# A graph kernel's edge sort with two half-float values per edge in place of one packed whole number in fp32

## The chip, the cores and the metric

One core of one Trainium2 chip runs the kernel. The metric is the device time of one execution in microseconds (us). A timed measurement is the median of several runs. TensorE (PE in the rows; PEld is its weight loading), VectorE (DVE), ScalarE (ACT), GpSimd (POOL) and SyncE (SP, which only issues transfers here) run side by side and meet at semaphores.

## What is computed

Four graph layers over 625 nodes of 512 features and 10625 edges (source, destination, a type 0 or 1, 64 edge features), each behind a layer norm and a ReLU, each added to x. The change touches only how the edges are brought into order by destination for the first two layers:

```python
def rgcn_gate_layer(x, row, col, edge_type, basis, att, gate_w, root, bias):
    w = jnp.einsum('rb,bio->rio', att, basis)
    x_j = x[col]
    ...
    msg = jnp.where((edge_type == 0)[:, None], msgs[0], msgs[1])
    agg = jax.ops.segment_sum(msg, row, num_segments=x.shape[0])
    return agg + x @ root + bias
x = x + _L0_gnn_ref(h, edge_index, edge_type_2, ...)   # two such layers, 30 basis matrices each
x = x + _L1_gnn_ref(h, edge_index, ...)                # GCN
x = x + _L2_gnn_ref(h, edge_index, edge_attr_64, ...)  # MLP per edge
x = x + _L3_gnn_ref(h, edge_index_t, ...)              # MLP per edge, no edge features
```

## The kernel before

The first phase (to about 465 us of the trace) does the two gated layers and the GCN. The sums over edges become products with count matrices (how many edges of a type go from node m to node n), and these are built on the chip in two steps.

**The sort.** The edges lie in 84 tiles of 128. DVE finds for each edge its place among the edges ordered by chunk of 128 destinations: a tile (0 to 87) and a slot in it (0 to 127). Then 84 fp32 matmuls move one number per edge there: for edge tile e the stationary operand `place_hots[e % 24]` (128x128, GpSimd, L716) has a one at the edge's slot, the moving operand `value_hots[e % VALUE_RING]` (128x88, DVE, `move_hots`, L740) has the edge's number in the column of its tile. All 84 add up in one PSUM bank, `PS[:, MOVE_BANK, 0:88]` (`sort`, L350). The number packs all three values: (1024 * type + source) * 256 + destination in the chunk + 1 (`places`, L788 to L794). `read_moved` (L743 to L758) takes it apart with seven DVE operations. `VALUE_RING` is 21 slots, in the space of `is_src`.

**The counting.** For each of the 87 sorted tiles DVE writes `is_slot` (128x128, L764) and `is_src` (128x640, L766) in half-float, and PE multiplies them (L369, L371).

**The order around it** is written by hand, one program per engine:

- PE runs `sort(0)` to `sort(83)`. After e = 2, 6, ..., 78 comes a `mix` (L393): four 32-column fp32 matmuls that combine the 30 basis matrices of layer 1 by one of 56 pieces of 1 MB. After e = 45, 49, ..., 61 there are four transposes of a chunk of the normed input (L399); after e = 67 the gates, `gates` (L405, 20 matmuls with 2 columns); after e = 73 and e = 80 a product with `root` (`product`, L411). Then come `clear` (L364) and the counting.
- DVE runs `move_hots(0)` to `move_hots(83)`, with other work put in after fixed e: the norm's statistics after 28, the normed rows after 36, `slots(0)` after 46, `chunks(1)` after 56, `pack_chunks` after 60, `places_without_gaps` after 66, `pairs_of_chunks` after 72, `chunks(0)` after 76 (L1061 to L1079).
- GpSimd writes the 84 `place_hots` and waits only for a free one of 24.
- ACT copies the mixes out of PSUM (L1272). SP loads piece n when mix n - 4 has ended (`load`, L610).

Of the kernel before, what the change touches and what calls it, by code (L numbers as in the profile page):

```python
# [8 lines left out]
F32 = mybir.dt.float32  # L9
F32R = mybir.dt.float32r  # L10
BF16 = mybir.dt.bfloat16
FP16 = mybir.dt.float16
# [5 lines left out]
P = 128  # L18
# [24 lines left out]
KIND = 1024.0  # L43
SPOT = 256.0
LOW = 1
# [6 lines left out]
def gnn_stack(nc, a, out):  # L52
    ctx = ExitStack()
    with ctx:
# [129 lines left out]
        with early:  # L184
# [52 lines left out]
            group_id = part(10)  # L237
            values = part(11)[:, 0:ET]
            by_chunk = part(12).rearrange("p (j t) -> p j t", j=4)
# [52 lines left out]
            PLACE_RING = 24  # L292
            VALUE_RING = HOT * NP // 2 // SC
            place_hots = packed[:].rearrange("p c n -> p (c n)")[:, 0:PLACE_RING * P].rearrange("p (b n) -> p b n", n=P)
            value_hots = is_src[:].rearrange("p b n -> p (b n)").bitcast(F32)[:, 0:VALUE_RING * SC].rearrange("p (b n) -> p b n", n=SC)
            EARLY_BANKS = (7, 0, 1)
# [26 lines left out]
            def _(pe):  # L323
# [22 lines left out]
                def sort(e):  # L346

                    pe.wait_ge(sem("place_hots"), e + 1)
                    pe.wait_ge(sem("one_hot"), e + 1)
                    nc.tensor.matmul(PS[:, MOVE_BANK, 0:SC], place_hots[:, e % PLACE_RING, :], value_hots[:, e % VALUE_RING, :],  # L350
                                     start=(e == 0), stop=(e == ET - 1), skip_group_check=True).then_inc(sem("hot_used"), 1)

                def clear(g):

                    if g:
                        pe.wait_ge(sem("packing"), NT * g)
                        pe.wait_ge(sem("packed"), NT * g)
                    else:
                        pe.wait_ge(sem("zeros"), 1)
                        pe.wait_ge(sem("rank_read"), 2)  # L360
                        pe.wait_ge(sem("by_chunk"), 7)
                        pe.wait_ge(sem("side_ev"), EARLY_SIDES)
# [4 lines left out]
                def count(t, c):  # L367
                    pe.wait_ge(sem("one_hot"), ET + 2 * t + 2)
                    nc.tensor.matmul(PS[:, bass.ds(c, 1), :].rearrange("p c o -> p (c o)"), is_slot[:, t % HOT, :], is_src[:, t % HOT, 0:512],  # L369
# [365 lines left out]
            def _(dve):  # L735
                def move_hots(e):

                    if e >= VALUE_RING:
                        dve.wait_ge(sem("hot_used"), e - VALUE_RING + 1)
                    nc.vector.tensor_scalar(value_hots[:, e % VALUE_RING, :], node_of_col[:, 0:SC], slot_tile[:, 1, e:e + 1],  # L740
                                            values[:, e:e + 1], ALU.is_equal, ALU.mult).then_inc(sem("one_hot"), 1)

                def read_moved():  # L743

                    moved = PS[:, MOVE_BANK, 0:SC]
                    dst_s, kind_s, src_s, weight_s = (by_chunk[:, j, :] for j in range(4))
                    dve.wait_ge(sem("hot_used"), ET)
                    nc.vector.tensor_scalar(src_s, moved, 1.0 / SPOT, -0.25, ALU.mult, ALU.add).then_inc(sem("by_chunk"), 1)
                    dve.wait_ge(sem("by_chunk"), 1)
                    nc.vector.tensor_scalar(src_s, src_s, ROUND, -ROUND, ALU.add, ALU.add).then_inc(sem("by_chunk"), 1)  # L750
                    dve.wait_ge(sem("by_chunk"), 2)
                    nc.vector.scalar_tensor_tensor(dst_s, src_s, -SPOT, moved, ALU.mult, ALU.add).then_inc(sem("by_chunk"), 1)
                    nc.vector.tensor_scalar(kind_s, src_s, KIND, None, ALU.is_ge).then_inc(sem("by_chunk"), 1)
                    dve.wait_ge(sem("by_chunk"), 4)
                    nc.vector.tensor_scalar(dst_s, dst_s, -1.0, None, ALU.add).then_inc(sem("by_chunk"), 1)
                    nc.vector.scalar_tensor_tensor(src_s, kind_s, -KIND, src_s, ALU.mult, ALU.add).then_inc(sem("by_chunk"), 1)
                    nc.vector.tensor_scalar(weight_s, kind_s, PACK - 1.0, 1.0, ALU.mult, ALU.add).then_inc(sem("by_chunk"), 1)
                    dve.wait_ge(sem("by_chunk"), 7)  # L758

# [26 lines left out]
                def places():  # L786

                    nc.vector.scalar_tensor_tensor(place[:], group, -float(P), ends[:], ALU.mult, ALU.add).then_inc(sem("place"), 1)  # L788
                    nc.vector.scalar_tensor_tensor(values, kind[:], KIND, ends[:, 0, :], ALU.mult, ALU.add).then_inc(sem("place"), 1)
                    dve.wait_ge(sem("place"), 2)  # L790
                    nc.vector.scalar_tensor_tensor(values, values, SPOT, place[:, 1, :], ALU.mult, ALU.add).then_inc(sem("values"), 1)
                    dve.wait_ge(sem("values"), 1)
                    nc.vector.tensor_scalar(values, values, 1.0, None, ALU.add).then_inc(sem("values"), 1)
                    dve.wait_ge(sem("values"), 2)  # L794

# [1416 lines left out]
```

## Time and profile before

| | us |
|---|---|
| median of 3 runs (lowest to highest) | 1159.91 (1156.43 to 1161.3) |
| the profiled execution's own time | 1161.15 |
| its span in the trace | 1159.4 |
| PE busy in the span | 1086.1 (94%) |
| DVE busy | 835.8 (72%) |
| GpSimd busy | 559.3 (48%) |
| first sort matmul to the first operation of `read_moved` | 25.4 to 103.7 |

The page of the profile lists busy times over the span, a table of slices, and the costliest groups. A row of the timeline gives the start, the time until the last of the merged instructions ended, the engine, the line, out<-in with shapes, the count, and in brackets the idle time of the engine before it with what ended it. An fp32 matmul stands in the trace as two PE records and two PEld records, a half-float one as one of each, so `L350 ... x8` is four sorts.

### The profile page before, as it was taken

The page shows a single profiled execution, that of the slowest core. Times are in us where ns is not written, and L with a number is a line of the kernel's source. Part 1 is how long each engine was busy: PE and PEld are TensorE (multiplying, and loading weights), DVE is VectorE, ACT ScalarE, POOL GpSimd, SP SyncE. Part 2 cuts the span into 40 slices and gives each one's busy share as a digit, 9 for nine tenths or more (in the row PEclk, how much of TensorE's full clock was granted, in tenths as well). Part 3 has the DMA queues.
Part 4 walks back from the last instruction along what each step waited for, and adds up shares of the span by engine and source line. Part 5 has one row for each costly group of instructions (what it writes and reads, how often), then busy time and mean ns, then how long its engine had stood idle before and what let it go on. Part 6 is the DMA issues. An engine that isn't in the chain of part 4 may idle for free. (4 is left out here: it accounts for less than half of the span.)

```text
span 1159.4 us, 15448 instructions
## 1 busy us (share of the span) xinstructions
PE 1086.1 (94%) x4410; PEld 607.0 (52%) x4442; DVE 835.8 (72%) x1852; ACT 558.3 (48%) x978; POOL 559.3 (48%) x518
## 2 busy tenths in 40 slices
PE   3989888899999989899999999999999999999997
PEld 1564222344557453655565565555555557446664
DVE  5694677769755153688788788788888867849997
ACT  0221321310332221477777777777777744116663
POOL 1960112233433330667876666666666300027774
PEclk9988989999999999899999999999999999999999
DMA  7995997657211005595554454445454010026665
GB/s 283 341 404 212 360 400 264 231 184 233 84 48 46 13 14 194 132 259 111 114 110 92 101 98 95 100 95 97 98 98 88 1 55 23 9 93 197 203 206 173
DMA packets 60182, 172.66 MB, mean 149 GB/s; under 512 B 12645, under 2 KB 13189, under 8 KB 52552
## 3 DMA queue, kind: packets, MB, share of 16 engines
q0 software_dynamic: 31536, 72.01, 26.6%
q1 hardware_dynamic: 28568, 99.66, 23.4%
q8 instruction: 42, 0.69, 0.2%
q14 instruction: 36, 0.29, 0.1%
HBM read 159.65 MB, written 11.98 MB: 148 GB/s over the span
## 5 line engine op out<-in xcount | busy, mean ns | idle before, releaser
L1664 PE MATMUL PS<-wide,hidT 128*128 128x512 f32 x672 | 302.1, 592 | 2.2 <-DVE hidT L1540 0.4
L705 POOL DMA_INDIRECT rec_scratch<-rec_src,slot_row x84 | 102.5, 1220 | 252.8 <-DMA rec_scratch<-rec_src,slot_row 208.2
L1664 PEld LDWEIGHTS PS<-wide,hidT 128*128 128x128 f32 x672 | 128.6, 191 | 122.8 <-issue 120.5
L1482 POOL DMA_INDIRECT pair_sum<-table_j,counts_rec x84 | 136.7, 1627 | 27.3 <-issue 25.3
L1598 ACT ACTIVATE wide<-PS 128x512 f32<-128x512 f32 x168 | 100.5, 598 | 99.6 <-PE PS L1648 63.5
L1801 POOL DMA_INDIRECT u_space<-table_j,wide x87 | 86.1, 990 | 108.7 <-DMA table_j<-agg_space 81.8
L1474 POOL DMA_INDIRECT pair_sum<-table_i,counts_rec x84 | 89.5, 1066 | 98.9 <-PE PS L1648 59.5
L1603 ACT ACTIVATE wide<-wide,two 128x512 f32<-128x512 f32 x168 | 120.9, 720 | 6.2 <-DVE wide L1533 6.2
L1533 DVE SCALAR_TENSOR_TENSOR wide<-wide 128x512 f32<-128x512 f32 x168 | 116.4, 693 | 5.8
L1491 POOL DMA_INDIRECT rec_scratch<-rec_src,slot_row x84 | 89.5, 1066 | 40.9 <-issue 21.6
L1608 ACT ACTIVATE wide<-wide 128x512 f32<-128x512 f32 x168 | 105.8, 630 | 5.3
L1540 DVE SCALAR_TENSOR_TENSOR hidT<-wide,PS 128x512 f32<-128x512 f32 x84 | 57.8, 688 | 54.0 <-ACT wide L1608 54.0
L1272 ACT COPY pieces<-PS 128x512 f32<-128x512 f32 x56 | 32.8, 586 | 122.4 <-PE PS L393 122.4
L393 PE MATMUL PS<-pieces,mixer 128*32 128x512 f32 x448 | 67.8, 683 | 22.6 <-DVE mixer L1053 13.8
L1648 PE MATMUL PS<-attr,w_attr 128*128 128x128 f32 x672 | 88.7, 275 | 0.0
L1531 DVE TENSOR_SCALAR wide<-wide 128x512 f32<-128x512 f32 x168 | 72.2, 430 | 20.9 <-ACT wide L1598 20.9
L1648 PEld LDWEIGHTS PS<-attr,w_attr 128*128 128x128 f32 x672 | 81.6, 192 | 0.0
L411 PE MATMUL PS<-w_rel,hT 128*128 128x512 f32 x160 | 71.7, 598 | 1.8 <-ACT pieces L1272 1.8
L1885 DVE TENSOR_TENSOR wide<-PS,u_space 128x512 f32<-128x512 f32 x87 | 59.9, 689 | 10.1 <-issue 4.3
L1553 DVE SCALAR_TENSOR_TENSOR mes<-wide,PS 128x512 f32<-128x512 f32 x84 | 57.8, 688 | 12.2 <-ACT wide L1608 2.7
L1645 PEld LDWEIGHTS PS<-ident,pair_sum 128*128 128x128 f32 x336 | 41.7, 140 | 44.3 <-issue 44.3
L716 POOL TENSOR_SCALAR packed<-node_of_col,wide 128x128 f32<-128x128 f16 x84 | 51.0, 631 | 23.3 <-DVE wide L862 23.3
(325 smaller groups left out, 1884.9 us busy)
## 6 DMA issues: line engine op xcount, KB each, us to landing
pieces<-basis_rows SPq DMA_DIRECT2D x56, 1024.0 KB, 7.5
ring<-basis_low SPq DMA_DIRECT2D x30, 256.0 KB, 6.4
w_scratch<-pieces SPq DMA_DIRECT2D x112, 32.0 KB
counts_rec<-rec_scratch SPq DMA_DIRECT2D x1, 2856.0 KB, 9.8
rec_scratch<-rec_src,slot_row POOLq DMA_INDIRECT x168, 2.3
root<-L_gnn_root SPq DMA_DIRECT2D x2, 1024.0 KB, 8.0
rows_in<-in_rows_in SPq DMA_DIRECT2D x2, 1024.0 KB, 13.9
w_rel<-w_scratch SPq DMA_DIRECT2D x1, 2048.0 KB, 11.6
```

What stands on the lines that cost most here:

```text
L705: nc.gpsimd.indirect_dma_start(out=rec3_dram, out_offset=bass.IndirectOffsetOnAxis(ap=slot_row[:, 1, t:t + 1], axis=0), in_=rec, in_offset ...
L1474: nc.gpsimd.indirect_dma_start(out=pair_sum[:, t % GOT3, :], out_offset=None, in_=tables[0][0], in_offset=bass.IndirectOffsetOnAxis(ap=idx ...
L1482: nc.gpsimd.indirect_dma_start(out=pair_sum[:, t % GOT3, :], out_offset=None, in_=tables[0][1], in_offset=bass.IndirectOffsetOnAxis(ap=idx ...
L1491: nc.gpsimd.indirect_dma_start(out=rec5_dram, out_offset=bass.IndirectOffsetOnAxis(ap=slot_row[:, 0, t:t + 1], axis=0), in_=rec5_src[:, t, ...
L1531: nc.vector.tensor_scalar(u, u, CLAMP, None, ALU.min).then_inc(sem(f"clamp{l}"), 1)
L1533: nc.vector.scalar_tensor_tensor(u, u, 2.0, u, ALU.add, ALU.mult).then_inc(sem(f"top{l}"), 1)
L1598: nc.scalar.activation(grow[l][:, t % 2, :], PS[:, bank, :], ACT.Exp).then_inc(sem(f"exp{l}"), 1)
L1603: nc.scalar.activation(u, u, ACT.Ln, bias=two[:]).then_inc(sem(f"ln{l}"), 1)
L1608: nc.scalar.activation(u, u, ACT.Exp, scale=-1.0).then_inc(sem(f"inv{l}"), 1)
L1648: m = nc.tensor.matmul(PS[:, pre_bank(t), k * P:(k + 1) * P], w_attr[:, k * P:(k + 1) * P], attr[:, t * P:(t + 1) * P], start=False, stop= ...
L1664: m = nc.tensor.matmul(o, hidT[:, t % 2, k * P:(k + 1) * P], w2[:, k, :], start=False, stop=(k == KT - 1), skip_group_check=True)
L1801: nc.gpsimd.indirect_dma_start(out=got5[:, t % GOT5, :], out_offset=None, in_=tables[1][1], in_offset=bass.IndirectOffsetOnAxis(ap=rec5[:, ...
```

## The change

`values` holds two rows per edge: row 0 is destination in the chunk + 1, row 1 is 1024 * type + source. Both are whole numbers that a half-float holds exactly. `value_hots` becomes half-float with 2 x 88 columns per edge tile, and `move_hots` writes the two halves with two instructions (L740 each); `VALUE_RING` stays 21. `place_hots` becomes half-float in the same bytes' space, written by the same 84 GpSimd instructions. `sort` becomes one half-float matmul with 176 moving columns in place of an fp32 one with 88. `read_moved` goes from seven operations to four, `places` from four to three. The semaphore counts follow.

```diff
@@ -41,7 +41,6 @@
 KIND = 1024.0
-SPOT = 256.0
 LOW = 1
@@ -235,7 +234,7 @@
             group_id = part(10)
-            values = part(11)[:, 0:ET]
+            values = part(11).rearrange("p (j t) -> p j t", j=2)
             by_chunk = part(12).rearrange("p (j t) -> p j t", j=4)
@@ -290,9 +289,9 @@
             PLACE_RING = 24
-            VALUE_RING = HOT * NP // 2 // SC
-            place_hots = packed[:].rearrange("p c n -> p (c n)")[:, 0:PLACE_RING * P].rearrange("p (b n) -> p b n", n=P)
-            value_hots = is_src[:].rearrange("p b n -> p (b n)").bitcast(F32)[:, 0:VALUE_RING * SC].rearrange("p (b n) -> p b n", n=SC)
+            VALUE_RING = HOT * NP // (2 * SC)
+            place_hots = packed[:].rearrange("p c n -> p (c n)").bitcast(FP16)[:, 0:PLACE_RING * P].rearrange("p (b n) -> p b n", n=P)
+            value_hots = is_src[:].rearrange("p b n -> p (b n)")[:, 0:VALUE_RING * 2 * SC].rearrange("p (b n) -> p b n", n=2 * SC)
             EARLY_BANKS = (7, 0, 1)
@@ -346,8 +345,8 @@
                     pe.wait_ge(sem("place_hots"), e + 1)
-                    pe.wait_ge(sem("one_hot"), e + 1)
-                    nc.tensor.matmul(PS[:, MOVE_BANK, 0:SC], place_hots[:, e % PLACE_RING, :], value_hots[:, e % VALUE_RING, :],
+                    pe.wait_ge(sem("one_hot"), 2 * e + 2)
+                    nc.tensor.matmul(PS[:, MOVE_BANK, 0:2 * SC], place_hots[:, e % PLACE_RING, :], value_hots[:, e % VALUE_RING, :],
                                      start=(e == 0), stop=(e == ET - 1), skip_group_check=True).then_inc(sem("hot_used"), 1)
@@ -358,14 +357,14 @@
                         pe.wait_ge(sem("rank_read"), 2)
-                        pe.wait_ge(sem("by_chunk"), 7)
+                        pe.wait_ge(sem("by_chunk"), 4)
                         pe.wait_ge(sem("side_ev"), EARLY_SIDES)
...
                 def count(t, c):
-                    pe.wait_ge(sem("one_hot"), ET + 2 * t + 2)
+                    pe.wait_ge(sem("one_hot"), 2 * ET + 2 * t + 2)
                     nc.tensor.matmul(PS[:, bass.ds(c, 1), :].rearrange("p c o -> p (c o)"), is_slot[:, t % HOT, :], is_src[:, t % HOT, 0:512],
@@ -737,25 +736,21 @@
                         dve.wait_ge(sem("hot_used"), e - VALUE_RING + 1)
-                    nc.vector.tensor_scalar(value_hots[:, e % VALUE_RING, :], node_of_col[:, 0:SC], slot_tile[:, 1, e:e + 1],
-                                            values[:, e:e + 1], ALU.is_equal, ALU.mult).then_inc(sem("one_hot"), 1)
+                    for j in range(2):
+                        nc.vector.tensor_scalar(value_hots[:, e % VALUE_RING, SC * j:SC * (j + 1)], node_of_col[:, 0:SC], slot_tile[:, 1, e:e + 1],
+                                                values[:, j, e:e + 1], ALU.is_equal, ALU.mult).then_inc(sem("one_hot"), 1)
...
-                    moved = PS[:, MOVE_BANK, 0:SC]
+                    moved = PS[:, MOVE_BANK, 0:2 * SC].rearrange("p (j t) -> p j t", j=2)
                     dst_s, kind_s, src_s, weight_s = (by_chunk[:, j, :] for j in range(4))
                     dve.wait_ge(sem("hot_used"), ET)
-                    nc.vector.tensor_scalar(src_s, moved, 1.0 / SPOT, -0.25, ALU.mult, ALU.add).then_inc(sem("by_chunk"), 1)
-                    dve.wait_ge(sem("by_chunk"), 1)
-                    nc.vector.tensor_scalar(src_s, src_s, ROUND, -ROUND, ALU.add, ALU.add).then_inc(sem("by_chunk"), 1)
+                    nc.vector.tensor_scalar(kind_s, moved[:, 1, :], KIND, None, ALU.is_ge).then_inc(sem("by_chunk"), 1)
+                    nc.vector.tensor_scalar(dst_s, moved[:, 0, :], -1.0, None, ALU.add).then_inc(sem("by_chunk"), 1)
                     dve.wait_ge(sem("by_chunk"), 2)
-                    nc.vector.scalar_tensor_tensor(dst_s, src_s, -SPOT, moved, ALU.mult, ALU.add).then_inc(sem("by_chunk"), 1)
-                    nc.vector.tensor_scalar(kind_s, src_s, KIND, None, ALU.is_ge).then_inc(sem("by_chunk"), 1)
+                    nc.vector.scalar_tensor_tensor(src_s, kind_s, -KIND, moved[:, 1, :], ALU.mult, ALU.add).then_inc(sem("by_chunk"), 1)
+                    nc.vector.tensor_scalar(weight_s, kind_s, PACK - 1.0, 1.0, ALU.mult, ALU.add).then_inc(sem("by_chunk"), 1)
                     dve.wait_ge(sem("by_chunk"), 4)
-                    nc.vector.tensor_scalar(dst_s, dst_s, -1.0, None, ALU.add).then_inc(sem("by_chunk"), 1)
-                    nc.vector.scalar_tensor_tensor(src_s, kind_s, -KIND, src_s, ALU.mult, ALU.add).then_inc(sem("by_chunk"), 1)
-                    nc.vector.tensor_scalar(weight_s, kind_s, PACK - 1.0, 1.0, ALU.mult, ALU.add).then_inc(sem("by_chunk"), 1)
-                    dve.wait_ge(sem("by_chunk"), 7)
@@ -786,12 +781,10 @@
                     nc.vector.scalar_tensor_tensor(place[:], group, -float(P), ends[:], ALU.mult, ALU.add).then_inc(sem("place"), 1)
-                    nc.vector.scalar_tensor_tensor(values, kind[:], KIND, ends[:, 0, :], ALU.mult, ALU.add).then_inc(sem("place"), 1)
+                    nc.vector.scalar_tensor_tensor(values[:, 1, :], kind[:], KIND, ends[:, 0, :], ALU.mult, ALU.add).then_inc(sem("place"), 1)
                     dve.wait_ge(sem("place"), 2)
-                    nc.vector.scalar_tensor_tensor(values, values, SPOT, place[:, 1, :], ALU.mult, ALU.add).then_inc(sem("values"), 1)
+                    nc.vector.tensor_scalar(values[:, 0, :], place[:, 1, :], 1.0, None, ALU.add).then_inc(sem("values"), 1)
                     dve.wait_ge(sem("values"), 1)
-                    nc.vector.tensor_scalar(values, values, 1.0, None, ALU.add).then_inc(sem("values"), 1)
-                    dve.wait_ge(sem("values"), 2)
```

On DVE the order stays, with two instructions where one stood. The place is the stretch from the 57th edge tile to the 73rd, around the other work that the prediction speaks of; L740 is `move_hots`, L980/L973 is `chunks(1)`, L809/L802 is `pack_chunks`, L873 to L896 (now L866 to L889) is `places_without_gaps`. Before:

```order
58 L980 SCALAR_TENSOR_TENSOR wide<-slot_of_col,wide 128x88 x3
59 L740 TENSOR_SCALAR is_src<-node_of_col,wide 128x88 x4
60 L807 COPY wide<-wide 128x11
61 L809 SCALAR_TENSOR_TENSOR wide<-wide 128x11 x7
62 L811 CAST words<-wide 1x11
63 L740 TENSOR_SCALAR is_src<-node_of_col,wide 128x88 x6
64 L873 MEMSET wide 128x6
```

With the change:

```order
57 L973 SCALAR_TENSOR_TENSOR wide<-slot_of_col,wide 128x88 x3
58 L740 TENSOR_SCALAR is_src<-node_of_col,wide 128x88 x8
59 L800 COPY wide<-wide 128x11
60 L802 SCALAR_TENSOR_TENSOR wide<-wide 128x11 x7
61 L804 CAST words<-wide 1x11
62 L740 TENSOR_SCALAR is_src<-node_of_col,wide 128x88 x12
63 L866 MEMSET wide 128x6
```

Four and six instructions became eight and twelve; nothing else moved.

On PE the order stays too. The place is the end of the sort, from the sort of e = 67 over the gates to the last one (L350/L349 `sort`, L405/L404 `gates`, L393/L392 `mix`, L411/L410 the root product). Before:

```order
52 L350 MATMUL PS<-is_src,packed 128x88
53 L405 MATMUL PS<-gate_cols,hT 128x2 x20
54 L350 MATMUL PS<-is_src,packed 128x88 x3
55 L393 MATMUL PS<-pieces,mixer 32x512 x4
56 L350 MATMUL PS<-is_src,packed 128x88 x3
57 L411 MATMUL PS<-root,hT 128x512 x4
```

With the change:

```order
52 L349 MATMUL PS<-is_src,packed 128x176
53 L404 MATMUL PS<-gate_cols,hT 128x2 x20
54 L349 MATMUL PS<-is_src,packed 128x176 x3
55 L392 MATMUL PS<-pieces,mixer 32x512 x4
56 L349 MATMUL PS<-is_src,packed 128x176 x3
57 L410 MATMUL PS<-root,hT 128x512 x4
```

The sorts have twice the columns in the same places.

## Rows read from the trace of the kernel before

**Rows 1.** The page: busy time of each engine over the span.
```profile
PE 1086.1 (94%) x4410; PEld 607.0 (52%) x4442; DVE 835.8 (72%) x1852; ACT 558.3 (48%) x978; POOL 559.3 (48%) x518
```

**Rows 2.** Stages: stretch, us, busy PE PEld DVE ACT POOL (last rows PE), PEclk, DMA, GB/s.
```profile
24.60:78.60 54.00, 45.19 (x292) 25.75 (x293) 42.53 (x143) 12.77 (x24) 51.73 (x85) 0.97 0.91 356
...
86.40:93.00 6.60, 6.60 (x24) 0.50 0.55 185
93.00:103.70 10.70, 10.70 (x51) 1.00 0.67 247
```

**Rows 3.** Timeline, DVE and POOL: the value and place one-hots.
```profile
24.58 8.15 DVE L740 TENSOR_SCALAR is_src<-node_of_col,wide 128x88 f32<-128x88 f16 x28
26.55 6.94 POOL L716 TENSOR_SCALAR packed<-node_of_col,wide 128x128 f32<-128x128 f16 x12
...
59.97 15.77 POOL L716 TENSOR_SCALAR packed<-node_of_col,wide 128x128 f32<-128x128 f16 x26
...
84.79 1.72 DVE L740 TENSOR_SCALAR is_src<-node_of_col,wide 128x88 f32<-128x88 f16 x7
```

**Rows 4.** DVE's busy time in the stretches of other work between the one-hots.
```profile
33.96:37.48 3.52, 3.49 (x13) 1.00 0.86 283
48.88:52.86 3.98, 3.84 (x10) 1.00 1.01 418
55.73:61.50 5.77, 5.29 (x16) 1.00 1.04 418
64.40:65.83 1.43, 1.29 (x5) 0.54 1.04 433
67.05:69.33 2.28, 2.00 (x10) 1.00 1.01 419
71.05:76.52 5.47, 4.94 (x17) 1.00 1.02 419
```

**Rows 5.** Timeline, PE and DVE: the last sorts and what follows them.
```profile
48.88 0.17 DVE L105 TENSOR_TENSOR small<-small 128x5 f32<-128x5 f32 x1 [8.39 <-ACT small L135]
...
77.39 1.06 PE L393 MATMUL PS<-pieces,mixer 128*32 128x512 f32 x8 [2.79 <-DMA pieces<-basis_rows]
...
78.67 7.97 PE L405 MATMUL PS<-gate_cols,hT 128*128 128x2 f32 x40
...
86.51 1.56 PE L350 MATMUL PS<-is_src,packed 128*128 128x88 f32 x6
...
91.24 4.51 PE L411 MATMUL PS<-root,hT 128*128 128x512 f32 x8
...
96.87 1.12 PE L350 MATMUL PS<-is_src,packed 128*128 128x88 f32 x8
...
99.44 3.63 PE L411 MATMUL PS<-root,hT 128*128 128x512 f32 x8
...
103.74 0.25 DVE L748 TENSOR_SCALAR wide<-PS 128x88 f32<-128x88 f32 x1 [17.23 <-PE PS L350]
```

**Rows 6.** Timeline, DVE and PE: half-float one-hots, and half-float matmuls.
```profile
105.18 0.25 DVE L764 TENSOR_SCALAR is_slot<-node_of_col,wide 128x128 f16<-128x128 f16 x1
105.35 0.44 DVE L766 TENSOR_SCALAR is_src<-node_of_col,wide 128x640 f16<-128x640 f16 x1
...
105.70 0.25 DVE L764 TENSOR_SCALAR is_slot<-node_of_col,wide 128x128 f16<-128x128 f16 x1
...
137.05 0.38 PE L369 MATMUL PS<-is_src,is_slot 128*128 128x512 f16 x1
...
137.32 0.38 PE L369 MATMUL PS<-is_src,is_slot 128*128 128x512 f16 x1
```

**Rows 7.** Groups by line: GpSimd beside the normed rows (48 to 53 us), and its memsets.
```profile
L716 POOL TENSOR_SCALAR packed<-node_of_col,wide 128x128 f32<-128x128 f16 x7 | 5.2, 773 | 0.0
...
L1795 POOL MEMSET none<- 128x512 bf16 x1 | 0.5, 547 | 0.0
L709 POOL MEMSET x_rows<- 128x512 f32 x1 | 0.5, 525 | 0.3 <-POOLq L2204 0.3
```

## The prediction

> **What bounds the kernel now.** I read the busy times first [rows 1]: PE is busy 94% of the span, so time won or lost where PE stands or works in the early stages mostly arrives at the end. Then the stages [rows 2]: in the first 54 us of the sort PE is busy 45.2 us, DVE 42.5 and GpSimd 51.7, with the DMA engines at 0.91. No single engine is the bound there, so the order of the program decides. The timeline of the sort's end [rows 5] gives the chain. PE ends the mix after e = 66 at 78.4 us, having waited 2.79 us for its piece of the basis; the gates start at 78.67 and take 7.97 us, 40 records of hardly any columns; the last 16 sorts, three mixes and two root products follow without a gap in PE's work, and `read_moved` starts at 103.74. Behind it stands everything else: PE clears the banks for the counting only when DVE has taken the sort's result apart.
>
> So two things can move 103.74: when PE may start the gates, and how long PE works behind them.
>
> **PE's side: cheaper sorts.** Behind the gates stand 16 sorts (e = 68 to 83). In fp32 three of them (six records) took 1.56 us at 0.50 of the granted clock, the level of 1.2 GHz, and four took 1.12 us at 1.00, which is 2.4 GHz [rows 2, 5]. That is about 0.50 and 0.25 us each, as the next work overlaps their ends. A half-float sort has 176 columns. Two pairs of half-float matmuls with 640 columns together start 0.27 us apart [rows 6], so 176 columns take 0.075 us at the least, and at the most the 0.25 of now. I take 0.10 at 2.4 GHz and 0.20 at 1.2 GHz, near the lower end, since the pair of those rows also holds two weight loads. Six sorts at the low clock win 6 x 0.30 = 1.8 us and ten at the high one 10 x 0.15 = 1.5: **3.3 us** on the path. The 68 sorts ahead of the gates get cheaper by the same amounts, 68 x 0.15 = 10 us or more. I cost that at nothing: PE will wait there for DVE, below, and if that cover goes, the mix after e = 66 is next, which waits for its DMA already.
>
> **`read_moved`** takes 103.74 to 105.18, 1.44 us for seven operations [rows 5, 6], 0.21 each. Four take 0.8: **0.6 us** won, on the path, as nothing else of DVE or PE can run. `places` loses one such operation of about 0.2 us. DVE waits behind it for PE's ranking, so I give it nothing; without that wait it would be 0.2.
>
> **DVE's side: twice the instructions.** This decides. Alone, `move_hots` starts every 0.235 us: 7 in 1.72 us, less the 0.31 that the last one takes to end, over 6 [rows 3]. For the new instruction the rows give two bounds. A half-float one-hot of 128 columns with one scalar per partition is followed by the next after 0.17 us, and the one of 640 columns with two scalars, the form of the new one, after 0.35 [rows 6]. So 88 columns cost at least 0.165 and at most the 0.235 of now. I take 0.21, near the upper end, since both scalars stay and nearly all of the 0.235 is fixed cost. An edge tile needs two, 0.42 us in place of 0.235.
>
> But GpSimd works beside it until 75.74 us (59.97 + 15.77), one place one-hot every 0.577 us (12 in 6.94, [rows 3]). There `move_hots` goes slower: 28 in 8.15 us, 0.286 each. That is two DVE instructions per GpSimd instruction, almost exactly: GpSimd holds DVE up once in each period, and the next two go through. Natural time for two is 0.47, so the hold costs 0.107. Does a third new instruction fit in a period? After the hold two of them take 0.42, and with the 0.107 of the hold the third would want to start at 0.53, some 0.05 ahead of GpSimd's next instruction. The hold must reach back from 0.107 behind GpSimd's start, by at least that. I hold it likelier that the third is caught than that it slips through. Then DVE keeps to two instructions per GpSimd instruction, which is now one edge tile: **0.577 us** in place of 0.286. GpSimd's own period I leave at 0.577: the write of 512 columns took it 525 ns in fp32 and 547 in two-byte numbers [rows 7].
>
> The sum for DVE, from 24.58 [rows 3] with the other work of [rows 4] as it stands: 29 tiles, 16.7, gives 41.3; statistics, 3.5, 44.8; 8 tiles 49.5; normed rows, 4.0, 53.4; 10 tiles 59.2; `slots(0)`, 5.8, 65.0; 10 tiles 70.7; `chunks(1)`, 1.4, 72.2; 4 tiles 74.5; `pack_chunks`, 2.3, 76.8. GpSimd is done now: 6 tiles at 0.42 give 79.3; `places_without_gaps`, 5.5, 84.8; the tile e = 67 comes at **85.2**. Today the same chain holds 8.39 us of waiting for ACT's part of the norm [rows 5], which hangs on PE's mix after e = 30. In the new one DVE comes there later than ACT, so that slack is eaten first; that is why the extra 68 x 0.29 us cost only a part of themselves. PE's gates start at 85.3 in place of 78.67: **6.6 us lost**.
>
> DVE's last 16 tiles, with `pairs_of_chunks` and `chunks(0)` between them, end at some 98 us, ahead of PE, which needs them behind its root products.
>
> **Sum:** + 6.6 - 3.3 - 0.6 = **+ 2.7 us** at the start of the counting. From there on PE, DVE, ACT, the loads and GpSimd's scatter all hang on that start, and I let the shift through to the end. The profiled execution took 1161.15 us, so the like of it would take 1163.9. It stands 1.24 above the median of 1159.91, so the median comes to **1162.5 us**. A measurement of this kernel can tell about 0.5%, 5.8 us, from no change.
>
> **The skill's rule.** By the Trainium skill (SBUF — State Buffer, Who interferes with whom) a DVE `tensor_scalar` in a two-port mode and a GpSimd instruction exclude each other for the whole instruction, whoever starts first. The trace agrees that they hold each other up, but not for the whole: two DVE instructions pass in each 0.577 us. Read literally it is the slow rival below.
>
> **Rivals.**
>
> *The third slips in* (0.30). If the hold reaches back less than 0.05 us, two GpSimd periods take five DVE instructions: 0.46 per tile. Of the 68 tiles up to e = 67, 61 then take 28.2 us and 7 take 2.9; with 22.45 of other work and 24.58 the gates start at 78.1. 78.67 - 78.1 + 3.3 + 0.6 = 4.5 us won: **1155.4**. For it: in the rows the hold is only seen 0.107 long. Against: it has never been seen to let a third through.
>
> *No hold that matters* (0.09). 68 x 0.42 = 28.6, the gates could start at 75.7, if the piece for the mix has landed: it came at 77.4, but the early mixes get quicker and so their loads are issued sooner. 3.0 + 3.9 = 6.9 us won: **1153**.
>
> *Longer holds on DVE's path: slower* (0.08). Place: `move_hots` beside L716. Beside the five wide DVE operations that norm the rows, GpSimd's instruction took 773 ns on average [rows 7], as the two engines pushed each other. With twice as many DVE instructions asking for the port the period may stretch likewise: at 0.773 per tile, 61 x 0.196 = 12 us on top, **1174.5**. If the two took strict turns, 1.15 per tile, it would be 35 us on top, 1198. It tells from 0.63 us per tile on, where the sum passes + 5.8.
>
> *The clock behind the gates* (0.11). Today it returns to 2.4 GHz at 93.0 [rows 2], within the first root product. That product took 4.51 us, the second 3.63 [rows 5]. PE would now idle for some six us ahead of the gates and has less work among them. If the whole first product ran at 1.2 GHz (7.3 us) and the mix behind it too, 2.8 + 0.9 = 3.7 us come on top: **1166**.
>
> *It stays as it was* in the remaining 0.42: 1162.5, give or take 2.
>
> **How the numbers follow.** Faster by over 0.5% (under 1154.1): most of the second rival and a sixth of the first, 0.14. Slower by over 0.5% (over 1165.7): the third rival, and some 0.08 of the clock and the upper edge of my own case: 0.16. The same: 0.70. The range reaches from the second rival to the clock's case with a margin, and leaves out half of the slow rival: 1153 to 1170.
>
> **What would show it.** Right: `move_hots` pairs 0.577 us apart while GpSimd runs, and 0.40 to 0.44 later; DVE no longer waiting 8.39 us for ACT; PE idle for DVE ahead of the gates, which start at 85; the last 16 sorts at 0.1 to 0.2 us each; `read_moved` starting near 106.4. Wrong: gates at 78 or sooner, GpSimd's mean for L716 over 650 ns, PE waiting for `place_hots`, or a difference that arises only behind the sort.

## The result and the profile after

The changed kernel takes 1162.26 us (median of 20 runs, 1159.73 to 1167.21) against 1159.28 for the kernel before, measured beside it: the ratio is 1.0032, with a 95% interval of 1.0017 to 1.0047. That is 2.0 to 5.5 us slower: clear of noise, and less than the 0.5% up to which the forecast called it the same. The forecast was 1162.5. The ratios leave out runs over 1.5% above the fastest of their kernel: there is one in this document, of kernel 8 below, at 2241.78 us. The profiled execution has a span of 1160.5 us, 1.1 above that of before.

The page, busy time of each engine over the span (against [rows 1]: DVE 18.1 us more, PE 9.7 less, GpSimd's half-float one-hots no cheaper to speak of):

```profile
PE 1076.4 (93%) x4358; PEld 589.5 (51%) x4358; DVE 853.9 (74%) x1932; ACT 558.1 (48%) x978; POOL 555.0 (48%) x518
```

Timeline of DVE and GpSimd, the value and place one-hots and the work between them (against [rows 3, 4, 5]):

```profile
24.53 16.48 DVE L740 TENSOR_SCALAR is_src<-node_of_col,wide 128x88 f16<-128x88 f16 x58
24.69 50.81 POOL L715 TENSOR_SCALAR packed<-node_of_col,wide 128x128 f16<-128x128 f16 x84 [23.25 <-DVE wide L855]
40.91 3.05 DVE L122 BATCH_NORM_STATS2 stats<-x_rows 128x6 f32<-128x512 f32 x5
44.42 4.70 DVE L740 TENSOR_SCALAR is_src<-node_of_col,wide 128x88 f16<-128x88 f16 x16
49.01 0.15 DVE L104 TENSOR_TENSOR small<-small 128x5 f32<-128x5 f32 x1
...
52.46 5.59 DVE L740 TENSOR_SCALAR is_src<-node_of_col,wide 128x88 f16<-128x88 f16 x20
57.97 0.15 DVE L833 TENSOR_SCALAR wide<-PS 128x6 f32<-128x6 f32 x1
...
64.34 5.70 DVE L740 TENSOR_SCALAR is_src<-node_of_col,wide 128x88 f16<-128x88 f16 x20
69.95 0.25 DVE L970 TENSOR_SCALAR wide<-slot_of_col,wide 128x88 f32<-128x88 f32 x1
...
71.42 1.92 DVE L740 TENSOR_SCALAR is_src<-node_of_col,wide 128x88 f16<-128x88 f16 x8
73.26 0.26 DVE L800 COPY wide<-wide 128x11 f32<-128x11 f32 x1
...
75.41 2.63 DVE L740 TENSOR_SCALAR is_src<-node_of_col,wide 128x88 f16<-128x88 f16 x12
77.99 0.06 DVE L866 MEMSET wide<- 128x6 f32 x1
...
82.81 2.64 DVE L740 TENSOR_SCALAR is_src<-node_of_col,wide 128x88 f16<-128x88 f16 x12
```

The first group's 58 instructions lie between 24.53 and 40.91: 0.282 us each, as in fp32. A tile needs two, so it costs 0.565. Behind 75.5, where GpSimd is done, it is 12 in 2.58 us: 0.215 each, 0.43 per tile. The wait of 8.39 us for ACT ahead of L104 has gone: ACT's part is there before DVE asks for it.

Timeline of PE and DVE at the end of the sort (against [rows 5, 6]):

```profile
78.35 1.06 PE L392 MATMUL PS<-pieces,mixer 128*32 128x512 f32 x8
83.47 0.31 PE L349 MATMUL PS<-is_src,packed 128*128 128x176 f16 x1 [4.05 <-DVE is_src L740]
83.59 8.67 PE L404 MATMUL PS<-gate_cols,hT 128*128 128x2 f32 x40
92.12 0.60 PE L349 MATMUL PS<-is_src,packed 128*128 128x176 f16 x3
92.65 1.94 PE L392 MATMUL PS<-pieces,mixer 128*32 128x512 f32 x8
...
94.94 5.28 PE L410 MATMUL PS<-root,hT 128*128 128x512 f32 x8
...
101.22 0.48 PE L349 MATMUL PS<-is_src,packed 128*128 128x176 f16 x4
101.63 1.06 PE L392 MATMUL PS<-pieces,mixer 128*32 128x512 f32 x8
...
106.69 0.25 DVE L748 TENSOR_SCALAR wide<-PS 128x88 f32<-128x88 f32 x1 [10.66 <-PE PS L349]
107.52 0.26 DVE L759 TENSOR_SCALAR is_slot<-node_of_col,wide 128x128 f16<-128x128 f16 x1
```

PE idles 4.05 us for DVE's e = 67 and starts the gates at 83.59 in place of 78.67. The counting's first `is_slot` is the mark that I follow through all runs below: 107.52 here, 105.18 before.

The stages show the clock (stretch, us, busy PE PEld DVE ACT POOL, PEclk, DMA, GB/s; against [rows 2]):

```profile
81.20:92.10 10.90, 8.63 (x41) 8.64 (x42) 10.04 (x49) 0.00 (x0) 0.00 (x0) 0.50 0.61 248
92.10:98.30 6.20, 6.20 (x19) 2.31 (x20) 3.83 (x18) 0.77 (x2) 0.00 (x0) 0.50 0.38 131
98.30:106.70 8.40, 8.35 (x39) 3.06 (x37) 0.01 (x1) 2.00 (x4) 0.00 (x0) 1.00 0.62 198
```

All of the gates, the mix behind them and 3.4 us of the root product ran at 0.50, which is 1.2 GHz; before, 2.4 GHz was back some two us into that product.

### The profile page after: what moved, and what is told of

Same layout as the page of the kernel before. It is cut to its first block and busy times, and to the rows that moved or that the text cites. A ratio compares the mean times of both kernels' runs of the same rounds, so it can differ in the third digit from the quotient of the medians.

```text
span 1160.5 us, 15392 instructions
## 1 busy us (share of the span) xinstructions
PE 1076.4 (93%) x4358; PEld 589.5 (51%) x4358; DVE 853.9 (74%) x1932; ACT 558.1 (48%) x978; POOL 555.0 (48%) x518
## 5 line engine op out<-in xcount | busy, mean ns | idle before, releaser
L704 POOL DMA_INDIRECT rec_scratch<-rec_src,slot_row x84 | 100.9, 1201 | 258.1 <-DMA rec_scratch<-rec_src,slot_row 211.1
L1484 POOL DMA_INDIRECT rec_scratch<-rec_src,slot_row x84 | 88.5, 1053 | 42.5 <-issue 21.3
L392 PE MATMUL PS<-pieces,mixer 128*32 128x512 f32 x448 | 68.8, 692 | 21.1 <-DVE mixer L1046 13.7
L410 PE MATMUL PS<-w_rel,hT 128*128 128x512 f32 x160 | 71.7, 598 | 1.9 <-ACT pieces L1265 1.8
L715 POOL TENSOR_SCALAR packed<-node_of_col,wide 128x128 f16<-128x128 f16 x84 | 50.8, 629 | 23.3 <-DVE wide L855 23.2
## 6 DMA issues: line engine op xcount, KB each, us to landing
w_rel<-w_scratch SPq DMA_DIRECT2D x1, 2048.0 KB, 10.8
```

The lines of the kernel that those rows point to most:

```text
L704: nc.gpsimd.indirect_dma_start(out=rec3_dram, out_offset=bass.IndirectOffsetOnAxis(ap=slot_row[:, 1, t:t + 1], axis=0), in_=rec, in_offset ...
L1484: nc.gpsimd.indirect_dma_start(out=rec5_dram, out_offset=bass.IndirectOffsetOnAxis(ap=slot_row[:, 0, t:t + 1], axis=0), in_=rec5_src[:, t, ...
```

## The experiments

The kernels of the experiments are called by their numbers. My theory: the doubled DVE instructions, each pair held up once by GpSimd's instruction, set the gates; the half-float sorts by themselves are a gain. The rivals were a cost of DVE's own that has nothing to do with GpSimd, and the order of the work around e = 67. Each ratio is to the kernel before.

**1. One DVE instruction again, with half-float sorts.** Both half-floats of an edge lie in one 32-bit word. DVE multiplies that word by one or zero, read as fp32, which keeps its bits, and PE reads the result as 176 half-floats. For an edge the upper half of the word is destination + 1, 1 to 128, so the word as fp32 is an ordinary number and never a denormal or a NaN; no other content was tried. The waits and the view of `read_moved` follow.

```diff
-                    for j in range(2):
-                        nc.vector.tensor_scalar(value_hots[:, e % VALUE_RING, SC * j:SC * (j + 1)], ...,
-                                                values[:, j, e:e + 1], ALU.is_equal, ALU.mult)
+                    nc.vector.tensor_scalar(word_hots[:, e % VALUE_RING, :], ...,
+                                            value_words[:, e:e + 1], ALU.is_equal, ALU.mult)
```

> The changed kernel with both half-floats of an edge packed into one 32-bit word, so that one DVE instruction per edge tile (fp32 words, as before the change) writes both; PE still gets 176 half-float columns. Theory 1 (DVE's second instruction, paired with GpSimd's port time, delays the gates): a tile costs 0.289 us again beside GpSimd, DVE stands ahead of PE at e = 67, the gates start at 76 to 78 us instead of 83.6, and with 23.1 us from there to the read-out as in the changed kernel the counting starts 4 to 5 us earlier than before the change: ratio 0.996 (0.9955 to 0.9975). Rival (the half-float matmuls or the clock behind them carry the loss): DVE's relief moves little, gates at 80 or later, ratio 1.000 to 1.003.

Measured: 1154.44 us, ratio 0.9945 (0.9926 to 0.9964). Its timeline, DVE and PE:

```profile
24.23 8.39 DVE L741 TENSOR_SCALAR is_src<-node_of_col,wide 128x88 f32<-128x88 f16 x29
44.98 0.17 DVE L104 TENSOR_TENSOR small<-small 128x5 f32<-128x5 f32 x1 [6.24 <-ACT small L134]
...
73.58 1.94 PE L394 MATMUL PS<-pieces,mixer 128*32 128x512 f32 x8 [3.72 <-DMA pieces<-basis_rows]
75.45 0.33 PE L351 MATMUL PS<-is_src,packed 128*128 128x176 f16 x1
75.57 8.60 PE L406 MATMUL PS<-gate_cols,hT 128*128 128x2 f32 x40
...
99.34 0.25 DVE L760 TENSOR_SCALAR is_slot<-node_of_col,wide 128x128 f16<-128x128 f16 x1
```

With the second instruction gone, ACT's wait is back, the gates come 8.0 us sooner than with the change, and they now hang on the DMA's piece. The gates came 0.4 us ahead of the 76 to 78 that I had said, `is_slot` 5.8 us ahead of the kernel before in place of 4 to 5, and the ratio lies just under its range. The half-float sorts, with the shorter `read_moved`, are a gain; the change paid it away, and more, on DVE.

**2. The other work moved behind.** In the changed kernel `places_without_gaps` stands after e = 68, not 66.

```diff
-                    if e == 66:
+                    if e == 68:
                         places_without_gaps()
```

> The changed kernel with places_without_gaps put in after e = 68 instead of 66, so that the tile e = 67, for which PE waits before the gates, comes before it. Theory 1: the 4.05 us of PE's wait for DVE there vanish, the gates start at 79.4 to 79.6 (when the mix after e = 66 has ended), DVE catches up during the gates, and the counting starts 4 us earlier than in the changed kernel, some 1.7 us earlier than before the change: ratio 0.9985. Rival (the time reappears as another wait for DVE behind the gates): the gates start earlier but the read-out stays at 105 to 106.7, ratio 1.001 to 1.003.

Measured: 1159.92 us, ratio 0.9994 (0.9980 to 1.0008); gates at 81.08, `is_slot` at 103.31. Against the change `is_slot` comes 4.2 us sooner, and the whole kernel takes 4.4 us less (1.0032 to 0.9994): so the cost is a wait of PE's, which an order can partly hide. The gates missed their 79.4 to 79.6: from 76.8 to 80.0 PE's granted clock was 0.50, and the mix at 77.37 took 1.94 us where the same one took 1.07 in the change.

**3. Both.** Edits 1 and 2 together.

> Both edits, packed words and the later place. Theory 1: with one instruction per tile DVE is no longer late at e = 67, so the later place adds nothing or under 1 us to the packed kernel: gates at 75 to 77, set by the piece for the mix after e = 66, ratio 0.995 to 0.997. Rival (places_without_gaps at its old place still holds the gates up in the packed kernel): 1 to 2 us better than the packed kernel alone.

Measured: 1154.86 us, ratio 0.9966 (0.9949 to 0.9982). PE waits 3.97 us for the piece ahead of the mix at 74.06, gates at 76.05, `is_slot` at 98.85. Nothing on top of edit 1, as DVE no longer sets the gates.

**4. A second DVE instruction in the kernel before.** Its result is not used; PE waits for both. Sorts and `read_moved` stay in fp32.

```diff
-                    pe.wait_ge(sem("one_hot"), e + 1)
+                    pe.wait_ge(sem("one_hot"), 2 * e + 2)
...
+                    nc.vector.tensor_scalar(counts_rec[:, ...], node_of_col[:, 0:SC], ...,
+                                            values[:, e:e + 1], ALU.is_equal, ALU.mult).then_inc(sem("one_hot"), 1)
```

> The kernel before the change, with a second, unused DVE instruction of the same form per edge tile (written to free space, and waited for by the sort): the change's cost for DVE without its gain for PE. Theory 1: a tile costs 0.577 us beside GpSimd and 0.47 alone, the gates start at 84 to 85, the stretch behind them is 25.1 us as before, and the counting starts 5 to 6 us later: ratio 1.0045 to 1.0055. Rival (fp32 sorts on PE hide part of the DVE delay, since PE was late itself): under 3 us, ratio 1.002 or less.

Measured: 1165.38 us, ratio 1.0050 (1.0030 to 1.0070). Its timeline, PE and DVE:

```profile
84.19 0.43 PE L350 MATMUL PS<-is_src,packed 128*128 128x88 f32 x2 [3.67 <-DVE counts_rec L742]
84.45 7.58 PE L405 MATMUL PS<-gate_cols,hT 128*128 128x2 f32 x40
...
96.24 3.63 PE L411 MATMUL PS<-root,hT 128*128 128x512 f32 x8
...
109.29 0.25 DVE L766 TENSOR_SCALAR is_slot<-node_of_col,wide 128x128 f16<-128x128 f16 x1
```

The doubling alone brings the gates to 84.45 and the wait on DVE. It is the loss of the change without its gains. From the gates to the end of the sort it took 23.4 us (84.45 to 107.86) against 25.1 before, with the same work: the clock had returned ahead of the root product. I had left that stretch as before, so `is_slot` came 4.1 us later and not 5 to 6.

**5. 60 of GpSimd's 84 instructions taken away.** It makes only the first 24 place one-hots, and the sorts wait for no more than these.

```diff
-                    pe.wait_ge(sem("place_hots"), e + 1)
+                    pe.wait_ge(sem("place_hots"), min(e + 1, PLACE_RING))
...
-                for e in range(ET):
-                    if e >= PLACE_RING:
-                        pool.wait_ge(sem("hot_used"), e - PLACE_RING + 1)
+                for e in range(PLACE_RING):
```

> GpSimd makes only the first 24 of the 84 place one-hots and every later sort takes one of those again, so the edges come out in wrong slots and the sums are of wrong pairs; every other instruction of the changed kernel stays. GpSimd is done with them near 39 us. Theory 1 (DVE pays 0.577 us per tile because GpSimd's instruction stops it once per period): the pairs of move_hots behind 39 us start 0.426 us apart, as they did alone at 82.81 us. 43 tiles times 0.151 = 6.5 us less for DVE, so DVE no longer sets the gates; the mix after e = 66 does, with its piece from the DMA, and the gates start at 76 to 78.5 in place of 83.6. The waiting for ACT's part of the norm comes back. The counting's first is_slot comes at 100 to 102.5 in place of 107.5, and the ratio to the kernel before is 0.995 to 0.999. Theory 2 (two half-float instructions with two scalars cost 0.28 us each in this stretch whatever GpSimd does, by DVE's own semaphores or by the DMA's traffic in SBUF): 0.56 us and more per tile also behind 39 us, gates at 83 to 84, is_slot at 107 to 108, ratio 1.003.

Measured: 1155.20 us, ratio 0.9965 (0.9953 to 0.9976). Its timeline, GpSimd, DVE and PE:

```profile
24.63 13.95 POOL L713 TENSOR_SCALAR packed<-node_of_col,wide 128x128 f16<-128x128 f16 x24 [23.19 <-DVE wide L853]
...
43.73 3.49 DVE L738 TENSOR_SCALAR is_src<-node_of_col,wide 128x88 f16<-128x88 f16 x16
51.11 4.34 DVE L738 TENSOR_SCALAR is_src<-node_of_col,wide 128x88 f16<-128x88 f16 x20
...
74.24 1.06 PE L392 MATMUL PS<-pieces,mixer 128*32 128x512 f32 x8 [1.73 <-DMA pieces<-basis_rows]
77.60 0.30 PE L349 MATMUL PS<-is_src,packed 128*128 128x176 f16 x1 [2.29 <-DVE is_src L738]
77.73 8.66 PE L404 MATMUL PS<-gate_cols,hT 128*128 128x2 f32 x40
...
101.06 0.25 DVE L757 TENSOR_SCALAR is_slot<-node_of_col,wide 128x128 f16<-128x128 f16 x1
```

The 20 instructions at 51.11 are followed by the next work at 55.36: 0.213 each, where the changed kernel took 5.51 us for the same 20. The hold is GpSimd's, and theory 2 has fallen. One part of theory 1 was wrong all the same: DVE still sets the gates. PE waits 1.73 us for the piece, and after that mix another 2.29 us for DVE's e = 67. Two instructions per tile are late there even where each costs only 0.213. The counterpart of `slots(0)`, 6.37 us in the changed kernel (57.97 to 64.34), took 5.08 here.

**6. A third DVE instruction in the changed kernel.** Its result is not used.

```diff
-                    pe.wait_ge(sem("one_hot"), 2 * e + 2)
+                    pe.wait_ge(sem("one_hot"), 3 * e + 3)
...
+                    nc.vector.tensor_scalar(counts_rec[:].bitcast(FP16)[:, ...], ...,
+                                            values[:, 1, e:e + 1], ALU.is_equal, ALU.mult).then_inc(sem("one_hot"), 1)
```

> The changed kernel with a third value instruction on DVE per edge tile, whose result nobody reads; PE waits for all three. Theory 1 (two DVE instructions per instruction of GpSimd, 0.213 us each alone): three take 1.5 periods, 0.866 us per tile, as long as GpSimd runs at its 0.577; GpSimd is 24 tiles ahead near 41 us and from there held back by its ring, so that it stops DVE once per tile: 0.75 to 0.87. The tile e = 67 is done at 96 to 101, the gates start there, DVE's last tiles end behind the second root product's start, is_slot comes at 119 to 125, and the ratio to the kernel before is 1.010 to 1.018. Theory 2 (the extra instruction is partly hidden, as the third slips into a period): 0.70 us per tile, gates at 91 to 93, is_slot at 114 to 117, ratio 1.006 to 1.009.

Measured: 1176.39 us, ratio 1.0141 (1.0121 to 1.0162). Its timeline, DVE and GpSimd:

```profile
24.69 31.80 POOL L715 TENSOR_SCALAR packed<-node_of_col,wide 128x128 f16<-128x128 f16 x55 [23.25 <-DVE wide L857]
...
27.38 0.32 DVE L742 TENSOR_SCALAR counts_rec<-node_of_col,wide 128x88 f16<-128x88 f16 x1
...
28.17 0.45 DVE L742 TENSOR_SCALAR counts_rec<-node_of_col,wide 128x88 f16<-128x88 f16 x1
...
29.11 0.32 DVE L742 TENSOR_SCALAR counts_rec<-node_of_col,wide 128x88 f16<-128x88 f16 x1
...
120.68 0.26 DVE L761 TENSOR_SCALAR is_slot<-node_of_col,wide 128x128 f16<-128x128 f16 x1
```

The third instruction of a tile comes 0.79 and 0.94 us after the last one, in turn: 1.73 for six instructions, three periods of GpSimd's 0.578 (55 in 31.8). Once the two engines are in step, two DVE instructions per instruction of GpSimd is what is granted, whatever they are used for. The gates began at 97.38, as theory 1 said.

**7. The gates ahead of the mix that waits.** From kernel 3: PE's mix of e = 66 stands after e = 68. The gates had relied on that mix's wait for ACT's last turned rows, so they get their own.

```diff
-            MIX_FIRST, MIX_SORT, MIX_COUNT = 2, range(2, 80, 4), ...
+            MIX_FIRST, MIX_SORT, MIX_COUNT = 2, tuple(e + 2 * (e == 66) for e in range(2, 80, 4)), ...
...
-                        gates(0, range(NT), early_side("G0"))
+                        bank = early_side("G0")
+                        pe.wait_ge(sem("side_ev"), side[("T0", NT - 1)] + 1)
+                        gates(0, range(NT), bank)
```

> The kernel with packed words and places_without_gaps after e = 68, and on PE the gates now stand ahead of the mix that waited for its piece: that mix moves from e = 66 to e = 68, behind the gates. In the trace before this step PE idled 3.97 us for the DMA at 74.06 and the gates began at 76.05. Theory 1 (once DVE keeps up, that DMA wait is what sets the end of the sort, and 8.6 us of gates can cover it): the gates begin near 70.5, the mix behind them no longer waits, read_moved begins at 94 to 95 in place of 98.01, is_slot at 95 to 96, and the ratio to the kernel before is 0.989 to 0.994. Theory 2 (the loads are the bound of this whole stretch; the two loads that were issued at 76.04 behind that mix are issued some 4 us later, and their pieces are then missing in the counting): is_slot at 95 to 96 all the same, but the lead is gone by the counting's first mixes, ratio 0.995 to 0.998. Theory 3 (the place or value one-hots of e = 68 to 83 come too late for PE): read_moved at 97 or later.

**8. Kernel 1 once more, on the same chip as 7.**

> The packed words by themselves once more, beside the same runs of the kernel before as the gates moved ahead, so that the two can be compared. Ratio 0.993 to 0.997 as in the first run; is_slot at 99 to 100.

Measured: kernel 7 takes 1147.54 us, ratio 0.9904 (0.9883 to 0.9925), kernel 8 1153.39, ratio 0.9958 (0.9937 to 0.9979), its `is_slot` at 98.42 (I had said 99 to 100). Kernel 7 is the fastest here, 1% ahead of the kernel before. Its timeline, PE and DVE:

```profile
69.00 5.70 PE L406 MATMUL PS<-gate_cols,hT 128*128 128x2 f32 x40
74.56 0.31 PE L351 MATMUL PS<-is_src,packed 128*128 128x176 f16 x1
74.80 1.94 PE L394 MATMUL PS<-pieces,mixer 128*32 128x512 f32 x8
...
79.25 3.67 PE L412 MATMUL PS<-root,hT 128*128 128x512 f32 x8
...
90.88 0.26 DVE L762 TENSOR_SCALAR is_slot<-node_of_col,wide 128x128 f16<-128x128 f16 x1
```

Theory 1 holds, and `is_slot` came 4 us sooner than it said. PE was at work right up to the gates, the granted clock stayed at 1.00 for their first 3.2 us, and they took 5.70 us where kernel 3's took 8.60, all at 0.50; the product took 3.67 in place of 4.22. This trace is of the fastest of kernel 7's six executions, 1142.12 us and 5.4 under their median, so its `is_slot` need not be the usual one.

**9 and 10. The same two moves on the kernel before and on the changed kernel.** The edits are those of 2 and 7.

> The kernel before, in fp32, with the two moves that the fastest version had: places_without_gaps after e = 68, and the gates ahead of the mix that waits for its DMA. DVE there spends one instruction per tile, as the packed words do, so its e = 67 is done near 71 us. Theory 1 (the gain of 1% came from the moves; the half-float sorts add only their 2 to 3 us behind the gates and the shorter read_moved): gates at 70.5 to 73, is_slot at 94 to 97, ratio 0.992 to 0.997. Theory 2 (the light half-float sorts are needed, as PE with fp32 sorts reaches e = 67 too late): gates at 75 or later, is_slot at 99 or later, ratio above 0.997.

> The changed kernel, with its two value instructions per tile, and the same two moves. DVE reaches e = 67 only at 77 us, as in the run with places_without_gaps later, so the gates cannot start before it. If DVE's doubled instructions are what sets the gates of the changed kernel: gates at 76 to 79, is_slot at 98 to 102, ratio 0.995 to 0.999, and the moves are worth 5 to 9 us less here than with packed words. If not: gates at 71 to 73 and the ratio of the packed version, 0.990.

Measured: 1153.00 us, ratio 0.9936 (0.9907 to 0.9964), for the kernel before with the moves, and 1157.61, ratio 0.9969 (0.9949 to 0.9988), for the changed one. Their timelines, PE:

```profile
74.43 4.56 PE L405 MATMUL PS<-gate_cols,hT 128*128 128x2 f32 x40
```

```profile
78.31 0.24 PE L349 MATMUL PS<-is_src,packed 128*128 128x176 f16 x1 [0.19 <-DVE is_src L742]
78.44 6.19 PE L404 MATMUL PS<-gate_cols,hT 128*128 128x2 f32 x40
```

In the changed kernel DVE's pairs hold the gates at 78.4, as was said: PE waits for DVE 5.41 us ahead of 64.85, 1.81 ahead of 75.76 and 0.19 right ahead of the gates. That the moves would be worth 5 to 9 us less there than with packed words was wrong: they took it from 1.0032 to 0.9969, 7.3 us, and the words from 0.9958 to 0.9904, 6.3. What stays is the distance between the two kernels, 7.5 us with the moves (0.9969 against 0.9904). In the kernel before neither theory was quite met: gates at 74.43, between the two, with no idle time of PE ahead of them since 53.0 us, as the fp32 sorts left it none to spare; by `is_slot` (97.19) and the ratio theory 1 is nearer. With the same moves the order is words 0.9904, fp32 0.9936, two half-float instructions 0.9969. Kernels 9 and 10 ran beside the same runs of the kernel before, with medians 4.6 us apart: the change costs about as much there (0.0033) as in the old order (0.0032). The lead of the words over fp32 with the moves (0.0032) is not clear of noise, as the two intervals overlap and were measured apart; without the moves it is (0.9945 and 0.9958 against 1).

**Does a shift at the sort's end reach the end of the kernel?** `is_slot` against before in the profiled executions, these executions' own times against the 1161.15 us of before, and the ratio taken times 1159.9 us:

| kernel | `is_slot`, us | that execution, us | whole kernel by the ratio, us |
|---|---|---|---|
| the change | +2.3 | +1.4 | +3.7 (2.0 to 5.5) |
| 1 words | -5.8 | -4.0 | -6.4 (-8.6 to -4.2) |
| 8 words again | -6.8 | -8.5 | -4.9 (-7.3 to -2.4) |
| 2 later | -1.9 | +2.1 | -0.7 (-2.3 to +0.9) |
| 3 words, later | -6.3 | -5.2 | -3.9 (-5.9 to -2.1) |
| 4 two in fp32 | +4.1 | +4.2 | +5.8 (3.5 to 8.1) |
| 5 GpSimd less | -4.1 | -5.6 | -4.1 (-5.5 to -2.8) |
| 6 three | +15.5 | +17.1 | +16.4 (14.0 to 18.8) |
| 7 gates first | -14.3 | -19.0 | -11.1 (-13.6 to -8.7) |
| 9 before, moves | -8.0 | -8.2 | -7.4 (-10.8 to -4.2) |
| 10 changed, moves | -3.9 | -2.3 | -3.6 (-5.9 to -1.4) |

Between 8 us of gain and 16 of loss it passes one to one within the intervals, or close to them (kernel 3 misses by 0.4). Single executions of one kernel scatter: 1 and 8 are the same kernel and differ by 0.9 us at `is_slot` and by 4.5 in their own times. Of the largest gain some 3 us did not arrive by the ratio, but the execution whose `is_slot` it is gained 19.0: this does not show that anything was lost on the way.

## Why the prediction was right

The forecast of 1162.5 was met by its own chain, with terms that were off and nearly cancelled. In the profiled executions the balance is +4.9 for the gates' start, +0.7 for the gates, -2.7 for PE behind them and -0.6 for `read_moved`: +2.3, where I had +6.6, nothing, -3.3 and -0.6: +2.7. The mechanism is the one I gave, but that the sum came so close is luck: I had put the gates' start 1.7 us too late, and the low clock's two terms that I had left out of the sum, 0.7 in the gates and 0.6 behind them, made up for most of that. And a shift that is known only as 2.0 to 5.5 us does not bear out a forecast to a few tenths.

- **The hold: confirmed.** Two DVE instructions per GpSimd instruction, 0.565 us per tile in the first group against 0.577, and 0.43 behind GpSimd's end against 0.42. Runs 4, 5 and 6 show it from both sides. The single starts in the changed kernel's trace show the step: from 26.2 to 40.9 us DVE's lie 0.21 and 0.37 us apart in turn, so the hold is some 0.15 and takes up what is left of the period. It needs a start-up: where a group begins, four gaps of 0.21 in a row pass unheld before the two are in step (52.72 to 53.57). In step GpSimd's own period stayed at 0.577 to 0.58, as I left it. By the Trainium skill's rule (SBUF — State Buffer, Who interferes with whom) the side that starts first has the shared port for its whole instruction. The runs agree on who disturbs whom (0.213 us without GpSimd, 0.282 with it) but not on the whole instruction: two of DVE's start in each of GpSimd's periods, and the strict turns that would have given 1198 did not occur.
- **The gates' start, mis-sized: +4.9 and not +6.6.** The 68 tiles took 36.9 us in place of 38.1 (from each group's start to the next work: 16.38, 4.59, 5.51, 5.61, 1.84, 2.58, and 0.43 for e = 67). A third instruction does slip through now and then, above all at 71.42, where only one of eight was held and they took 1.84 us, 0.23 each (the rival *The third slips in*, in a small part). The other work took 21.8 us in place of 22.45 (3.51, 3.45, 6.37, 1.47, 2.15 and 4.82), mostly as `places_without_gaps` ran behind GpSimd's end (77.99 to 82.81, 4.8 against 5.5). I had carried durations over from rows that stood beside GpSimd.
- **PE behind the gates, mis-sized: -2.7 and not -3.3.** The sorts gave what I said: three took 0.53 us at 1.2 GHz (0.18 each) and four 0.41 at 2.4 (0.10 each), starts taken to the next work's. But the product took 5.28 us, 0.77 more than before, and the gates, all at 0.50, took 0.7 more. That is the rival *The clock behind the gates*, which I had as a case apart at + 3.7: it came true by 1.5 us of the product and the gates. I had said nothing of the gates' own time.
- **`read_moved`: right,** 0.83 us against 0.8.
- **ACT's wait eaten first: right.** It is 8.39 us before, none in the changed kernel, and 6.24 again in run 1.
- **The early sorts at nothing: right.** PE waits for DVE there, 5.48 us ahead of 65.12 and 1.88 ahead of 76.06. What was named as next came true as well: in run 1, with the cover gone, the mix of e = 66 waits 3.72 us for its DMA.
- **One to one to the end: right** in the table, for a shift of this size.

## What to carry to other kernels

Count instructions before columns: DVE's one-hots of 88 columns started every 0.213 us here and those of 640 every 0.35, so a short one is mostly fixed cost. A second one per tile beside GpSimd cost a whole slot, 0.28 us, while PE's saving on the first 68 of 84 sorts lay under a wait. When two small numbers must be moved exactly, one 32-bit word that DVE masks and PE reads as two half-floats gives the cheap matmul without the second instruction. And once a wait is found ahead of a long run of work that doesn't depend on it, move that work in front: with the other move it took 7.4 us off the kernel before (run 9), twice what the change cost.

## What was not expected of the hardware

- 40 matmuls of two columns took 4.56 us (run 9), 5.70 (run 7), 6.19 (run 10), 6.36 (run 2), 7.58 (run 4), 7.97 (before), 8.60 (runs 1, 3 and 8), 8.66 (runs 5 and 6) and 8.67 (the change), for the same work, by when the granted clock fell from 1.00 to 0.50. In the runs from 8.60 on it had fallen before the gates began (in the change at 81.2 us, inside PE's wait of 4.05 for DVE), in run 9 it fell behind them, and in the others within them. Where PE had waited 0.57 us or less right ahead of the gates or of the mix before them, they took at most 6.36, where it had waited 2.29 us or more, at least 7.58. But a wait right ahead is not all of it: run 4 had idled 3.67 us and took 7.58, and in run 7 the clock fell 3.2 us into the gates although PE's last wait had ended at 67.61. What sets the moments of its fall and return was not settled. Run 7's gates, PE (stretch, us, busy PE, PEclk, DMA, GB/s):

```profile
69.00:72.00 3.00, 3.00 (x31) 1.00 1.01 421
72.40:74.60 2.20, 2.20 (x12) 0.50 1.04 415
```

- DVE multiplies a word that holds two half-floats by 1.0 or 0.0 without changing its bits where the word is an ordinary fp32 number (run 1), so a mask in fp32 can carry packed data.
